# Two conditioned attention layers: batches pipelined over half-query sub-groups, scores from float32r pieces on row halves

## The chip, the cores and the metric

The kernel runs on one core of a Trainium2 chip. The metric is the device time of one execution in microseconds. The median of three runs of the kernel before is 675.55 us (675.35 to 675.59).

## The reference

Two layers run one after the other on x, of 2 batches x 1024 tokens x 256 channels in float32. The first is softmax attention with 16 heads of 16 channels, the second a linear attention with 8 heads of 32 channels.

```python
# layer 0, 16 heads of 16
xn = layer_norm(x, norm_w, norm_b)
q, k = heads(xn @ q_w + q_b), heads(xn @ k_w + k_b)
att = softmax(einsum('bnhl,bmhl->bnmh', q, k) + (1 - mask) * -1e6, axis=2)
v = heads((xn @ v_w + v_b) * mask)
y = einsum('bnmh,bmhl->bnhl', att, v)
scale, shift = split(silu(cond) @ emb_w + emb_b)
x = x + silu(layer_norm(y) * (1 + scale) + shift) @ out_w + out_b
# layer 1, 8 heads of 32
xn = layer_norm(x, ln_w, ln_b)
q = softmax(heads(xn @ Wq + bq), axis=-1)
k = softmax(heads(xn @ Wk + bk + (1 - mask) * -1e6), axis=tokens)
v = heads((xn @ Wv + bv) * mask)
y = q @ (k.T @ v)                       # per head
x = x + silu(layer_norm(y) * (1 + scale1) + shift1) @ W_out + b_out
```

## The kernel before

The program is written engine by engine; each engine runs its own list in the order in which it is written, and semaphores join the lists. All DMAs are issued by SyncE's queue (SPq).

**Preparation.** For both batches in turn: the input norm on VectorE (`layer_norm`, L708 statistics, L722 normalise), transposes on TensorE (L491), scale and bias on ScalarE (L391, into `hT`), then the q and k projections of 4 head groups (L500, 128x512 float32 matmuls; `product` is the helper with line 500 for all projections) and the values. Each q,k unit is split into three bfloat16 pieces: ScalarE L406, VectorE L788, ScalarE L408, GpSimd L356. SPq writes the pieces of a group to DRAM (L297, L304) and reads them back as `qs` and `ks` (L280 to L282, the function `stack`), so that six products of pieces, the mask rows and the row maxima stand under each other in one operand of 102 rows.

**Attention.** There are 8 groups (2 batches x 4 groups of 4 heads). For each group the maxima of the scores are found first: 64 matmuls of 99 rows x 512 columns (L519) into two PSUM banks `sN`, and 64 VectorE reductions of 128x512 out of PSUM (L749). The negated maxima are transposed (L528), split (L738 to L744) and brought by DMA into the last rows of `qs` (`load_max`, L288 and L290), so that the next matmul, L581, gives scores minus maximum. Its 128x1024 unit is turned by ScalarE into probabilities (L425, `prob`), and L539 multiplies these with the values, four 32-column tiles of the array at a time, in float32. While group g is attended, the maxima of group g+1 are found: `ring_plan` spreads them between the score matmuls. The maxima of group 0, and half of those of group 1, come before the first score (`prologue`). L433 copies the sums, L524 transposes them, L757 and L759 divide.

**After the attention.** Layer norm, the output projection and the whole of layer 1 run stage by stage, both batches in turn in each stage; L851 adds into `xs`, and SPq stores `xs` (L329). The projection of `cond` (L552) is made in the last group.

## Time and profile before

| | us |
|---|---|
| median of the runs | 675.55 |
| span of the profiled execution | 674.4 |
| start to the first score's exponential | 110 |
| attention, to the last values | 414 |
| the rest of layer 0 and layer 1, to the end | 151 |
| TensorE busy | 589.8 |
| VectorE busy | 470.1 |
| ScalarE busy | 347.5 |

Times of single instructions come from the one profiled execution. A matmul in the trace lasts from its start to the end of its way through the array, so in a stream neighbours overlap: what one costs there is the distance between starts. A float32 matmul appears as two instructions.

### The profile page before, as it was taken

What the parts mean: (1) busy time and instruction counts of PE and PEld (TensorE: products, weight loads), DVE (VectorE), ACT (ScalarE), POOL (GpSimd) and SP (SyncE); (2) the same over time, 40 slices, a digit from 0 to 9 for tenths busy, and PEclk for the clock granted to TensorE, in tenths of its full rate; (3) what the DMA queues carried; (4) which work ended last, traced back from release to release, by engine and by line L of the source; (5) the groups of instructions that cost most, each with busy time, mean ns of one, the idle gap of its engine ahead of it and who ended that gap; (6) DMA issues with size and microseconds to landing.
All of it is one profiled execution on the core that took longest, in us unless ns stands there. A gap on an engine that the chain in (4) does not pass through costs nothing.

```text
span 674.4 us, 9341 instructions
## 1 busy us (share of the span) xinstructions
PE 589.8 (87%) x2922; PEld 241.6 (36%) x2922; DVE 470.1 (70%) x905; ACT 347.5 (52%) x409; POOL 53.5 (8%) x42
## 2 busy tenths in 40 slices
PE   1989888999999999999999999999889666999666
PEld 1464412222222222222222222222234553588655
DVE  4639996888788788788888788888020547585652
ACT  1565304564655656656656655656976421538021
POOL 7224600000000000000000000000000005000000
PEclk9999955999999999999999999999989896999969
DMA  8188801500600600600410330100000000000003
GB/s 228 51 142 205 338 21 31 65 0 4 96 1 3 95 0 3 93 2 3 70 25 3 52 43 3 57 7 3 2 1 1 0 0 1 0 1 1 0 1 124
DMA packets 20021, 29.95 MB, mean 44 GB/s; under 512 B 5202, under 2 KB 11556, under 8 KB 19844
## 3 DMA queue, kind: packets, MB, share of 16 engines
q1 hardware_dynamic: 19996, 29.62, 20.8%
q8 instruction: 15, 0.25, 0.2%
q14 instruction: 10, 0.08, 0.0%
HBM read 21.02 MB, written 8.60 MB: 44 GB/s over the span
## 4 chain that ended last, share of the span: by engine, by line
PE 62%; DVE 23%; ACT 9%; issue 4%; DMA 1%; SPq 0%; DVEq 0%; ACTq 0%
PE bank L539 18%; PE bank L519 15%; DVE halfmax L749 15%; PE bank L500 14%; PE bank L581 11%; ACT work L391 3%; DVE stats L708 2%; ACT work L425 2%; DVE y_all L788 1%; PE bank L552 1%; DVE work L722 1%; DVE parts L722 1%; PE bank L524 1%; ACT parts L408 1%; DMA vecs<-in_mask_BxS_ff 1%
## 5 line engine op out<-in xcount | busy, mean ns | idle before, releaser
L749 DVE TENSOR_REDUCE halfmax<-bank 128x1 f32<-128x512 f32 x512 | 325.7, 688 | 63.7 <-PE bank L519 63.5
L425 ACT ACTIVATE work<-bank 128x1024 f32<-128x1024 f32 x256 | 250.0, 1023 | 152.6 <-PE bank L581 152.3
L519 PE MATMUL bank<-ks,qs 99*128 (+1 forms) x512 | 202.9, 404 | 17.1 <-DVE halfmax L749 11.0
L581 PE MATMUL bank<-qs,ks 102*128 (+1 forms) x512 | 167.6, 386 | 7.9 <-ACT work L425 5.4
L539 PE MATMUL bank<-work,vs 128*32 128x512 f32 x1024 | 137.0, 608 | 0.4 <-ACT yT L433 0.4
L519 PEld LDWEIGHTS bank<-ks,qs 99*128 (+1 forms) x512 | 49.7, 97 | 228.4 <-DVE halfmax L749 125.3
L581 PEld LDWEIGHTS bank<-qs,ks 102*128 (+1 forms) x512 | 47.5, 100 | 61.2 <-ACT work L425 18.5
L500 PE MATMUL bank<-parts,work 128*128 128x256 f32 x192 | 44.6, 393 | 7.1 <-ACT work L391 7.1
L500 PEld LDWEIGHTS bank<-parts,work 128*128 128x128 f32 x192 | 37.7, 198 | 13.4 <-ACT work L391 7.6
L367 POOL COPY vs<-v_all 128x512 f32 (+1 forms) x8 | 4.9, 612 | 396.8 <-PE bank L539 396.8
L500 PE MATMUL bank<-work,y_all 128*128 128x512 f32 x64 | 30.9, 624 | 2.4 <-ACT work L391 2.4
L539 PEld LDWEIGHTS bank<-work,vs 128*32 128x32 f32 x1024 | 20.4, 108 | 34.2 <-issue 30.8
L851 DVE TENSOR_TENSOR xs<-xs,bank 128x512 f32<-128x512 f32 x16 | 11.0, 687 | 26.5 <-PE bank L500 26.5
L788 DVE SCALAR_TENSOR_TENSOR y_all<-bank,cols,parts 128x512 f32<-128x512 f32 x16 | 12.0, 749 | 15.2 <-ACT parts L406 15.2
L384 ACT ACTIVATE std<-var 128x8 f32<-128x8 f32 x8 | 1.7, 209 | 39.9 <-DVE var L713 39.9
L500 PE MATMUL bank<-work,parts 128*128 128x512 f32 x32 | 15.9, 653 | 6.7 <-ACT work L391 6.7
L356 POOL TENSOR_TENSOR parts<-y_all,parts 128x512 f32 x16 | 18.5, 1155 | 37.7 <-ACT parts L408 37.7
L491 PE MATMUL bank<-ident,parts 128*128 128x128 f32 x48 | 9.1, 366 | 13.7 <-DVE parts L722 12.5
L500 PE MATMUL bank<-wo,work 128*128 128x256 f32 x64 | 16.0, 413 | 4.5 <-ACT work L391 4.5
L391 ACT ACTIVATE work<-bank,modB,modA 128x512 f32<-128x512 f32 x16 | 11.1, 777 | 16.4 <-PE bank L491 16.4
L826 DVE TENSOR_TENSOR emb<-bank,cols 128x8 f32<-128x8 f32 x2 | 0.2, 162 | 27.2 <-PE bank L552 27.2
L491 PE MATMUL bank<-ident,work 128*128 128x128 f32 x80 | 11.3, 303 | 8.1 <-DVE work L722 7.4
(119 smaller groups left out, 406.1 us busy)
## 6 DMA issues: line engine op xcount, KB each, us to landing
part_rows<-parts SPq DMA_DIRECT2D x8, 768.0 KB, 5.0
qs<-part_rows SPq DMA_DIRECT2D x48, 128.0 KB
ks<-part_rows SPq DMA_DIRECT2D x48, 128.0 KB
xs<-in_x SPq DMA_DIRECT2D x2, 1024.0 KB, 6.1
out_x<-xs SPq DMA_DIRECT2D x4, 512.0 KB, 2.9
parts<-in_L_cond_emb_w SPq DMA_DIRECT2D x1, 1024.0 KB, 5.6
parts<-in_L_cond_W_emb SPq DMA_DIRECT2D x1, 1024.0 KB, 7.9
ks<-in_mask_BxSx_fk SPq DMA_DIRECT2D x1, 1024.0 KB, 4.8
```

The source lines that it names most:

```text
L356: pool.tensor_tensor(parts[:, b * HG + hg, 2, n * HALF:(n + 1) * HALF], rest[:, u % 2, :], parts[:, b * HG + hg, 1, n * HALF:(n + 1) * HAL ...
L391: act.activation(hT[b][:, kc, q * HALF:(q + 1) * HALF], B8[i], func, scale=A(kc), bias=Bc(kc)).then_inc(turn_read, 1)
L425: act.activation(prob[:, c % 2, j, :], sT[u % 2][:, :], ACT.Exp).then_inc(exp_done, 1)
L491: last = pe.transpose(o[:, t * P:(t + 1) * P], z[:, 4 * q + t, kc * P:(kc + 1) * P], ident[:, :])
L500: last = pe.matmul(o, l, r, start=(i == 0), stop=(i == len(terms) - 1))
L519: pe.matmul(o, qs[0:ROW_MAX, slot, j, qt * P:(qt + 1) * P], ks[0:ROW_MAX, slot, j, n * HALF:(n + 1) * HALF], start=True, stop=True).then_i ...
L539: last = pe.matmul(acc[32 * j:32 * j + 32, n * HALF:(n + 1) * HALF], vs[:, c, j, :], prob[:, c % 2, j, n * HALF:(n + 1) * HALF], start=(c ...
L581: last = pe.matmul(sT[u % 2][:, n * HALF:(n + 1) * HALF], ks[0:ROWS, slots[0], j, c * P:(c + 1) * P], qs[0:ROWS, slots[0], j, n * HALF:(n ...
L708: dve.bn_stats(stats[:, b, t, :], src(t)).then_inc(ln_step, 1)
L722: dve.tensor_scalar(dst, s, mv[:, b, t, 0:1], rstd[:, b, t:t + 1], op0=ALU.subtract, op1=ALU.mult).then_inc(z_ready, 1)
L749: dve.tensor_reduce(halfmax[:, r, n:n + 1], src, axis=AX.X, op=ALU.max, negate=True).then_inc(sN_read, 1)
L788: dve.scalar_tensor_tensor(out=rest[:, u % 2, :], in0=B8[4 + u % 4], scalar=cols[:, c:c + 1], in1=parts[:, b * HG + hg, 0, n * HALF:(n + 1 ...
```

## The change

The program is rewritten around one loop of 128 steps.

- **Pieces.** q and k are split into two float32r pieces instead of three bfloat16 ones: ScalarE writes the first, VectorE the second, and GpSimd no longer takes part. Three products of pieces, two mask rows and two maximum rows make 52 rows (50 for the maxima), so a head fits into 64 partitions. Heads 0 and 2 of a group lie on partitions 0 to 63 of `qs` and `ks`, heads 1 and 3 on 64 to 127, and matmuls come in pairs, one on each half, into two banks. A piece is float32 in DRAM; a group is brought in by 20 DMAs instead of 13.
- **Sub-groups.** A group is cut into two halves of 512 queries. A sub-group has 8 steps, one for each 128 keys; a step holds two score pairs (L782), two 128x1024 exponentials, the values of the step before (L799) and four matmuls for the maxima (L682), which run 40 maxima ahead. The counts of all of these are those of the kernel before: 512 score matmuls, 512 maxima, 256 exponentials, 512 value matmuls. The ring of banks for maxima and all side work has three banks instead of two; the value sums have one.
- **Pipelining.** Only batch 0 is prepared before the loop. The preparation of batch 1, the projection of `cond`, and, once the groups of batch 0 are done, the rest of layer 0 and all of layer 1 for batch 0 are placed in single steps by the table `begins`; a projection is cut into two parts, one in each half of a step. Behind the loop stands batch 1's rest of layer 0 and layer 1.
- **Moved work.** The square root of the norms becomes a power on GpSimd, which also normalises four of the eight norms (L503). Biases of queries and values are added by a matmul with ones (L667) instead of VectorE. In the loop, SiLU is one 128x2048 instruction of its own (L564).
- The maxima go straight from SBUF to `qs` by two DMAs, without DRAM. SPq issues the first of these after the stacks of groups 1 and 2 and the weights of layer 1.

The core of the diff:

```diff
-    Q_PART = [0, 0, 0, 1, 1, 2]
-    K_PART = [0, 1, 2, 0, 1, 0]
-    PARTS = 3
+    Q_PART = [0, 0, 1]
+    K_PART = [0, 1, 0]
+    PARTS = 2
+    TILE = P // 2
+    SUBS = G * NH
+    STEPS = SUBS * NT
+    QT = HALF // P
+    MAXES = GH * QT * NH
+    AHEAD = MAXES + 8
...
+        stream = [("max", s, m) for s in range(SUBS) for m in range(MAXES)]
+        def maxima(k, p):
+            at = AHEAD + 4 * k + 2 * p
+            return stream[at:at + 2]
+        for (hg, n), k in zip([(hg, n) for hg in range(HG) for n in range(NH)], (4, 5, 7, 8, 19, 20, 21, 23)):
+            begins["qk", 1, hg, n] = (k, 0)
+        for s, k in enumerate((10, 11, 12, 13)):
+            begins["v", 1, s] = (k, 0)
+        for l in range(2):
+            begins["emb", l] = (15 + l, 0)
+            begins["embT", l] = (17 + l, 1)
+        for s in range(SUBS - 1):
+            begins["y", s] = (NT * (s + 1) + 1, 1)
+            begins["neg", s + 1] = (NT * (s + 1) - 2, 0)
...
+        for u, k in enumerate((88, 90, 91, 92)):
+            begins["keys", 0, u] = (k, 0)
+        for s, k in enumerate((93, 95, 96, 98)):
+            begins["queries", 0, s] = (k, 0)
+        for s, k in enumerate((99, 100, 101, 103)):
+            begins["values", 0, s] = (k, 0)
...
+        pe_first = [("T", "in0", 0, i) for i in range(4)] + [("qk", 0, hg, n) for hg in range(2) for n in range(NH)]
+        pro_rest = [("qk", 0, 2, 0), ("qk", 0, 2, 1), ("qk", 0, 3, 0), ("qk", 0, 3, 1)] + [("v", 0, s) for s in range(4)]
+        pe_beside, dve_beside = [], []
+        for i in range(AHEAD):
+            if i % 4 == 3 and i // 4 < len(pro_rest):
+                pe_beside.append(pro_rest[i // 4])
+            pe_beside.append(stream[i])
+            if i == MAXES + 1:
+                pe_beside.append(("neg", 0))
+            dve_beside.append(stream[i])
+            if i % 4 == 1 and 1 <= i // 4 and pro_rest[i // 4 - 1:] and pro_rest[i // 4 - 1][0] == "qk":
...
-            for g in range(HG):
-                sp.wait_ge(part3_ready, (g + 1) * NH)
-                sp.dma_start(part_rows[g], parts[:, g]).then_inc(parts_out, 16)
-                if g < 2:
-                    sp.wait_ge(parts_out, 16 * (g + 1))
-                    stack(g, g)
-                    sp.wait_ge(stack_in, (g + 1) * 16 * STACKS)
-            for g in range(HG, G):
-            load_max(0, 0)
...
+                    sp.wait_ge(rows_ready, 4 * (slot + 1))
+                else:
+                    sp.wait_ge(sT_ready, 2 * NT * NH * (g - SLOTS + 1))
+                sp.wait_ge(parts_out[g % 2], 16 * (g // 2 + 1))
+                for two in range(2):
+                    for r, part in enumerate(Q_PART):
+                        src = part_rows[g, 0:GC, part, :].rearrange("(c two p) n -> two p c n", two=2, p=DH0)[two]
+                        for n in range(NH):
+                            sp.dma_start(qs[two * TILE + r * DH0:two * TILE + (r + 1) * DH0, slot, n, :, :].bitcast(F32),
+                                         src[:, :, n * HALF:(n + 1) * HALF]).then_inc(stack_in[slot], 16)
+                    for r, part in enumerate(K_PART):
+                        src = part_rows[g, GC:2 * GC, part, :].rearrange("(c two p) n -> two p c n", two=2, p=DH0)[two]
+                        sp.dma_start(ks[two * TILE + r * DH0:two * TILE + (r + 1) * DH0, slot, :, :].bitcast(F32), src).then_inc(stack_in[slot], 16)
...
+            store_parts(0)
+            stack(0)
+            sp.dma_start(wo0[:, :, :], out_w.rearrange("(k p) c -> p k c", p=P)).then_inc(wo_in, 16)
             for i, src in enumerate((emb_w, W_emb)):
                 sp.dma_start(embw[:, i], src.rearrange("(e p) c -> p e c", p=P)).then_inc(embw_in, 16)
+            for g in range(1, HG):
+                store_parts(g)
+            stack(1)
+            stack(2)
             for i, src in enumerate((Wq, Wk, Wv, W_out)):
+                sp.dma_start(w1[:, i], src.rearrange("(k p) c -> p k c", p=P)).then_inc(w1_in, 16)
+            load_mrow(0)
+            load_max(0)
+            for k in range(STEPS):
+                for g in range(HG, G):
+                    if k == begins["qk", 1, g % HG, 1][0] + 2:
+                        store_parts(g)
+                if k % NT == NT - 2 and k // NT + 1 < SUBS:
+                    load_max(k // NT + 1)
+                if k % (NT * NH) == 0 and SLOTS <= k // (NT * NH) + 2 < G:
+                    stack(k // (NT * NH) + 2)
...
-                            last = pe.matmul(sT[u % 2][:, n * HALF:(n + 1) * HALF], ks[0:ROWS, slots[0], j, c * P:(c + 1) * P],
-                                             qs[0:ROWS, slots[0], j, n * HALF:(n + 1) * HALF], start=True, stop=True)
-                            if n == NH - 1:
-                                last.then_inc(sT_ready, 1)
...
+            def scores(k, u):
+                s, g, n, c = where(k)
+                if u == 0 and c == 0:
+                    pe.wait_ge(cmax_in, 32 * (s + 1))
+                if k > 0:
+                    pe.wait_ge(exp_done, 2 * (k - 1) + u + 1)
+                for two in range(2):
+                    rows = slice(two * TILE, two * TILE + ROWS)
+                    last = pe.matmul(sT[u][:, two * HALF:(two + 1) * HALF], ks[rows, g % SLOTS, u, c * P:(c + 1) * P],
+                                     qs[rows, g % SLOTS, n, u, :], start=True, stop=True)
+                last.then_inc(sT_ready, 1)
...
+                for j in range(GH):
+                    last = pe.matmul(acc[32 * j:32 * j + VW, :], vp[:, b, c, hg * GH + j, :], prob[:, c % 2, j, :],
+                                     start=(c == 0), stop=(c == NT - 1), skip_group_check=True)
...
+            for k in range(STEPS):
+                scores(k, 0)
+                for key in maxima(k, 0):
+                    fill(key, 0)
+                for key, part in pe_at[k, 0]:
+                    fill(key, part)
+                scores(k, 1)
+                if k > 0:
+                    values(k - 1)
+                for key in maxima(k, 1):
+                    fill(key, 0)
+                for key, part in pe_at[k, 1]:
+                    fill(key, part)
...
-                    pe.matmul(o, qs[0:ROW_MAX, slot, j, qt * P:(qt + 1) * P], ks[0:ROW_MAX, slot, j, n * HALF:(n + 1) * HALF],
-                              start=True, stop=True).then_inc(sN_ready, 1)
...
+                    rows = slice(two * TILE, two * TILE + ROW_MAX)
+                    last = pe.matmul(o, qs[rows, g % SLOTS, n, c, t * P:(t + 1) * P], ks[rows, g % SLOTS, c, half * HALF:(half + 1) * HALF], start=True, stop=True)
...
+                for kc in range(KC):
+                    last = pe.matmul(o[:, part * D:(part + 1) * D], hT[:, kc, at], w[:, kc, :], start=(kc == 0), stop=(kc == KC - 1 and row is None))
+                if row is not None:
+                    last = pe.matmul(o[:, part * D:(part + 1) * D], ones[:, :], brow[:, row, :], start=False, stop=True)
...
-                    dve.scalar_tensor_tensor(out=rest[:, u % 2, :], in0=B8[4 + u % 4], scalar=cols[:, c:c + 1],
-                                             in1=parts[:, b * HG + hg, 0, n * HALF:(n + 1) * HALF],
-                                             op0=ALU.add, op1=ALU.subtract).then_inc(pj_read, 1)
...
+                    dve.scalar_tensor_tensor(out=staged[:, 1, :].bitcast(F32R), in0=o, scalar=cols[:, COL["qk_b"] + hg:COL["qk_b"] + hg + 1], in1=staged[:, 0, :],
+                                             op0=ALU.add, op1=ALU.subtract).then_inc(u.done, 1)
...
-                    pool.tensor_tensor(parts[:, b * HG + hg, 2, n * HALF:(n + 1) * HALF], rest[:, u % 2, :],
-                                       parts[:, b * HG + hg, 1, n * HALF:(n + 1) * HALF], op=ALU.subtract).then_inc(part3_ready, 1)
...
+                for t in range(NT):
+                    pool.tensor_scalar(z[:, t, :], source(kind, b, t), rstd[:, L, t:t + 1], shift[:, L, t:t + 1], op0=ALU.mult, op1=ALU.add).then_inc(z_ready[kind, b], 1)
...
+                    act.activation(hT[:, :, :], hT[:, :, :], ACT.Silu).then_inc(silu_ready[key[1:]], 1)
```

TensorE inside the attention of the kernel before (L519 maxima, L581 scores, L539 values):

```order
L519 MATMUL bank<-ks,qs 128x512
L581 MATMUL bank<-qs,ks 128x512 x2
L519 MATMUL bank<-ks,qs 128x512
L581 MATMUL bank<-qs,ks 128x512
L519 MATMUL bank<-ks,qs 128x512
L539 MATMUL bank<-work,vs 32x512 x4
```

TensorE in a step of the changed kernel with no side work but the transposes of finished values (L682 maxima, L782 scores, L799 values, L691 transposes):

```order
L782 MATMUL sT<-qs,ks 128x512 x2
L682 MATMUL bank<-ks,qs 128x512 x2
L782 MATMUL sT<-qs,ks 128x512 x2
L799 MATMUL bank<-prob,vp 17x512 x4
L682 MATMUL bank<-ks,qs 128x512 x2
L691 MATMUL bank<-ident,yT 128x128 x4
```

The single maxima between scores have become pairs, and four matmuls of the maxima, four of the scores and one block of values still make a step.

TensorE in step 10 of the changed kernel, where values of batch 1 are projected (L665 with `wv`, L667 the bias):

```order
L782 MATMUL sT<-qs,ks 128x512 x2
L682 MATMUL bank<-ks,qs 128x512 x2
L665 MATMUL bank<-wv,hT 128x256 x2
L667 MATMUL bank<-brow,ones 128x256
L782 MATMUL sT<-qs,ks 128x512 x2
L799 MATMUL bank<-prob,vp 17x512 x4
L682 MATMUL bank<-ks,qs 128x512 x2
L665 MATMUL bank<-wv,hT 128x256 x2
L667 MATMUL bank<-brow,ones 128x256
```

In the kernel before, projections stood ahead of the attention; six float32 matmuls of 256 columns now stand among the scores of one step.

SPq before the first maxima DMA, in the kernel before (from the stack of group 1 on):

```order
L280 DMA qs<-part_rows 16x4x1024 x6
L280 DMA ks<-part_rows 16x4x1024 x6
L282 DMA ks<-mask_rows 3x4x1024
L297 DMA part_rows<-parts 128x3072 x2
L304 DMA part_rows<-parts 128x3072 x4
L308 DMA parts<-in_L_cond_emb_w 128x4x512
L308 DMA parts<-in_L_cond_W_emb 128x4x512
L310 DMA parts<-in_L_cond_Wq 128x2x256
L310 DMA parts<-in_L_cond_Wk 128x2x256
L310 DMA parts<-in_L_cond_Wv 128x2x256
L310 DMA parts<-in_L_cond_W_out 128x2x256
L288 DMA max_rows<-cparts 32x3x128
```

SPq in the changed kernel, from behind the stack of group 0 to the first maxima DMA (L420); the second of the two stacks, with the same rows as the first, and the last three weights are not shown:

```order
L442 DMA late<-in_L_cond_W_emb 128x4x512
L394 DMA part_rows<-late 128x2048 x3
L407 DMA qs<-part_rows 16x2x512 x6
L411 DMA ks<-part_rows 16x2x1024 x3
L412 DMA ks<-mask_rows 2x2x1024
...
L448 DMA w<-in_L_cond_Wq 128x2x256
...
L427 DMA late<-in_mask_BxSx_fk 128x1024
L420 DMA qs<-crows 2x8x128 x4
```

Two whole stacks, 40 DMAs, and five large loads now stand ahead of the first maxima.

## Rows read from the trace of the kernel before

**Rows 1.** The page: busy time, share of the span and instructions of each engine.

```profile
PE 589.8 (87%) x2922; PEld 241.6 (36%) x2922; DVE 470.1 (70%) x905; ACT 347.5 (52%) x409; POOL 53.5 (8%) x42
```

**Rows 2.** Busy time by stretch; columns as the first line says.

```profile
core 0: us, PE busy (x) PEld busy (x) DVE busy (x) ACT busy (x) POOL busy (x), PEclk, DMA share, GB/s
97.00:109.00 12.00, 10.04 (x19) 1.96 (x19) 10.78 (x20) 0.03 (x1) 0.00 (x0) 0.50 0.02 5
109.00:523.00 414.00, 391.70 (x2092) 110.28 (x2090) 301.76 (x530) 259.68 (x267) 4.29 (x7) 0.99 0.18 27
...
221.51:274.82 53.31, 50.56 (x266) 13.83 (x265) 43.62 (x74) 32.13 (x33) 0.62 (x2) 1.00 0.22 31
```

**Rows 3.** Timeline of two score units, mid attention: start, duration, engine, line, idle before.

```profile
250.20 0.39 PE L519 MATMUL bank<-ks,qs 99*128 x1
...
250.52 1.06 PE L539 MATMUL bank<-work,vs 128*32 128x512 f32 x8
...
251.51 0.39 PE L519 MATMUL bank<-ks,qs 99*128 x1
...
251.74 0.38 PE L581 MATMUL bank<-qs,ks 102*128 x1
...
251.94 2.54 DVE L749 TENSOR_REDUCE halfmax<-bank 128x1 f32<-128x512 f32 x4 [0.54 <-PE bank L519]
251.96 0.38 PE L519 MATMUL bank<-ks,qs 99*128 x1
251.96 0.32 PEld L581 LDWEIGHTS bank<-qs,ks 102*128 x2
252.18 0.60 PE L581 MATMUL bank<-qs,ks 102*128 x2
252.59 1.94 ACT L425 ACTIVATE work<-bank 128x1024 f32<-128x1024 f32 x2 [1.07 <-PE bank L581]
...
253.61 1.06 PE L539 MATMUL bank<-work,vs 128*32 128x512 f32 x8
```

**Rows 4.** Groups by form: count, busy us, mean ns of one, idle before.

```profile
L749 DVE TENSOR_REDUCE halfmax<-bank 128x1 f32<-128x512 f32 x512 | 325.7, 688 | 63.7 <-PE bank L519 63.5
...
L500 PE MATMUL bank<-parts,work 128*128 128x256 f32 x192 | 44.6, 393 | 7.1 <-ACT work L391 7.1
...
L500 PE MATMUL bank<-work,y_all 128*128 128x512 f32 x64 | 30.9, 624 | 2.4 <-ACT work L391 2.4
...
L356 POOL TENSOR_TENSOR parts<-y_all,parts 128x512 f32 x16 | 18.5, 1155 | 37.7 <-ACT parts L408 37.7
...
L788 DVE SCALAR_TENSOR_TENSOR y_all<-bank,cols,parts 128x512 f32<-128x512 f32 x16 | 12.0, 749 | 15.2 <-ACT parts L406 15.2
...
L500 PE MATMUL bank<-att,qs 128*128 128x128 f32 x32 | 3.7, 275 | 0.0
...
L673 PE MATMUL bank<-ident,parts 128*128 128x128 f32 x16 | 1.9, 272 | 0.0
```

**Rows 5.** Waits of SPq from 26 to 47 us: total, times, longest.

```profile
SPq L297 <- DMA ks<-mask_rows: 7.6, 1, 7.6
...
SPq L280 <- DMA part_rows<-parts: 2.9, 1, 2.9
```

**Rows 6.** Timeline of the start, SPq: start, duration of the issues.

```profile
29.23 0.36 SPq L297 DMA_DIRECT2D part_rows<-parts  x1
32.51 2.69 SPq L280 DMA_DIRECT2D qs<-part_rows  x6
35.24 2.77 SPq L280 DMA_DIRECT2D ks<-part_rows  x6
```

**Rows 7.** The chain that ended last, behind the attention: start, duration, what.

```profile
527.73 1.28 ACT L391
529.03 2.80 ACT work L391 x4
531.87 8.86 PE bank L500 x32
...
544.04 7.19 PE bank L500 x32
551.94 2.63 DVE stats L708 x8
555.96 2.67 DVE parts L722 x8
```

1344 lines of the change are left out of this document (699 added, 645 removed).

## The prediction

> **What bounds the kernel now.** I read the shares of the engines first: TensorE is busy for 87% of the span, VectorE for 70% [rows 1]. The stretches then say where: the attention takes 414 us of the 674.4 [rows 2], and a steady group in it 53.3 us, of which TensorE is busy 50.6, VectorE 43.6 and ScalarE 32.1. The timeline of two score units [rows 3] says what one round costs. From one values block to the next are 3.09 us. The block takes 0.99 to the start of the next matmul, and its start comes 0.32 after the maximum before it, 0.10 more than the 0.22 between neighbours: 1.09 with the change of tile shape. Eight bfloat16 matmuls at 0.22 make 1.76. So TensorE has 2.85 of work, and the missing 0.24 is time in which VectorE had not yet freed one of two banks. VectorE needs 2.51 for its four reductions (four take 2.54, the last 0.03 of it is latency; 0.627 each), ScalarE 1.94 for two exponentials. TensorE is the bound, VectorE stands 0.34 behind it.
>
> **The attention step.** Counts stay: per step four maxima, four score matmuls, one values block, two exponentials. What changes on TensorE is that the eight matmuls become four pairs on row halves. No row shows float32r, nor a matmul on half the rows. Bounds for a pair: 0.22, if a float32r piece streams like bfloat16 and the halves run together, as the four column tiles of a values block do (eight instructions of 512 columns in 0.99); 0.44, if one half follows the other; and 0.95, if they follow each other at the rate of a float32 transpose, one pass of 128 columns in 0.119 [rows 4] or 0.475 for 512. I take 0.25, near the lower end, because the tiles of the values block are the nearest rows for two tiles at a time, and because the trace's plain float32 matmul shows two instructions where float32r has one. TensorE then has 4 x 0.25 + 1.09 = 2.09 in a step, and VectorE with 2.51 becomes the bound. Two engines then stand close, so a wait remains; with three banks I take half of the 0.24 of [rows 3], 0.12, with 0 and 0.24 as its ends.
>
> A page speaks against the pairs: the Trainium skill, "TensorE: Matmul & The Clock Gate", Part 3, says that a weight load overlaps a matmul in flight only when their row groups differ. The trace disagrees for whole rows: a load of 102 rows begins at 251.96 together with a matmul of 99 rows [rows 3], and two loads take 0.32, the second starting 0.22 after the first, so 0.10 each. By the rule a pair would take 0.22 + 0.10 = 0.32, a quiet step 2.37 on TensorE, still below 2.51, and the steps bound by TensorE together some 11 us more.
>
> **Side work in the loop.** Prices: a float32 matmul of 256 columns is two instructions of 0.225 (32 in 7.19 us, [rows 7]; 0.232 in [rows 4]), so 0.45, one of 512 columns 0.9, one of 128 columns 0.23 (3.7/32 twice), a transpose 0.12 [rows 4]. For each of the 128 steps I add what the table puts there on TensorE, VectorE and ScalarE, and take the largest:
> - 84 steps without projections: VectorE, 84 x 2.51 = 211, and 46 us of its small work in them (finishing the maxima, dividing y, statistics, splits at 0.75 [rows 4]): 257.
> - 20 steps with a projection of two 512-column matmuls, or four of 256: TensorE 2.09 + 1.8 = 3.9 (less in the last four, which have no maxima): 77.
> - 12 steps with layer 0 or layer 1 values, or queries: six matmuls of 256, because of the bias matmul, 2.09 + 2.7 = 4.8: 57.
> - 5 steps with the projection of `cond`, the k.T v product or y: 26.
> - 2 steps with the SiLU: 128x2048 on ScalarE, 1.9 by the exponential's rate, and two table loads of 1.28 [rows 7], beside 1.9 of exponentials, 6.3 each: 13.
> - 5 steps without maxima or projections: ScalarE, 13.
> Sum 443. To it: 128 x 0.12 = 15 of waits. Batch 1's first norm: statistics, then GpSimd's power and its eight normalising instructions (half of the 1.155 of a 512-column one each, [rows 4]), stand in steps 1 to 3, while TensorE's transposes in steps 2 and 3 already wait for them, with all later scores queued behind: about 5. Every float32 projection between pairs adds two changes of tile shape; about 110 fall into steps that TensorE bounds. Between 0 and 0.10 each, I take 0.04: 5. The loop is 443 + 15 + 5 + 5 = 468.
>
> The Trainium skill, "TensorEngine Tiling (Array Packing)", Key Properties, says that each change of the tiling mode drains the engine. At the 0.10 of [rows 3] the 110 changes would cost 11 instead of 5, which would make the loop 474.
>
> **Ahead of the loop.** Until the first q,k unit little changes. The third piece is gone, two stages of a unit less, so the store of group 0 goes out at about 26 instead of 29.2 [rows 6] and lands 3 to 4 later (2.9 of waiting behind a 0.36 issue, [rows 5], for 768 KB; now 1 MB). The stack of group 0 took 13.6 us before, from 32.5 to 46.1 (issues to 38.4, 7.6 of waiting, [rows 5, 6]). Its bytes are the same, 1.5 MB, its issues are 20 at 0.45 = 9. I take 12 to 13: the first maximum runs at about 43. Then 40 maxima with 8 projections: four rounds of 0.75 + 2.51 on VectorE (13) and four on TensorE of 2.7 + 1.1 (15), then 5 for the rest: 78, the maxima of the first sub-group being ready at 76. But SPq stores group 3 only after its last q,k unit, at 57, then issues two stacks (40 x 0.45 = 18) and the five loads (3): the first maxima DMA is issued at 78. In front of it in the same queue lie 3.2 MB of stacks at 12 to 13 per stack, hence until 57 + 25 = 82, and 1.5 MB of loads, 4 to 6. First score at 88, between 80 and 94, against 110 before. All engines idle for that wait; it is new.
>
> **Behind the loop.** One batch instead of two, so its latencies are bare:
> - last values, copy 1.0, transposes, division: 3; statistics 2.6 [rows 7], aggregation 1.1, power 0.7, half a normalisation 1.3, transposes, table load 1.3, two ScalarE units 1.4: 9.
> - output projection 8.9, the cold one of [rows 7] (the second, 7.2).
> - add, statistics, norm, ScalarE: 7. Keys 8.6.
> - Queries and values 2 x 24 matmuls x 0.45 = 21.6, transposes 3.9, k.T v 32 x 0.23 / 2 = 3.7, waits 1, y 3.7: 34.
> - norm 8, projection 8.9, add and the store 4.5.
> Sum 92, of which some 3 overlap: 89, between 82 and 97.
>
> The span is 88 + 468 + 89 = 645, and with the 1.15 by which the median stands above the span of the profile, 646: 0.956 of before.
>
> **The rivals.**
> - The halves don't run together, or stream at half the rate together: a pair costs 0.44. For it: no row shows two row groups at work. Then TensorE stays the bound with 4 x 0.44 + 1.09 = 2.85 in a step, exactly as before, and the projections come on top of it. The largest of each step sum to 486; with waits of 0.12 to 0.24 and the 10 above, 511 to 527, total 689 to 705. Slower by 2 to 4%. It decides from a pair of about 0.37 up: each 0.01 of a pair above 0.35 costs 3 to 5 us.
> - float32r streams at the transpose's rate, one half after the other, 0.95 a pair: TensorE's sum is 492 pairs x 0.95 + 128 x 1.09 + 99 of side work = 706, total near 890.
> - The waits are as large as now, and the first score is at 94: 646 + 15 + 6 = 667. Same direction, half the gain.
> - Everything tight: pairs at 0.22, no waits, no drains, the start at 82 and the end at 84: 441 + 5 + 166 + 1 = 613.
> - The clock. The granted clock fell to 0.50 where TensorE only waited between single maxima from 97 to 109 us [rows 2]; it stayed at 0.99 in the attention. A step with 2.09 of work in 2.63 lies between the two. At half clock a quiet step costs 4.2 on TensorE and the loop over 680, but TensorE would then be busy throughout, so I give it little.
>
> **How the numbers follow.** The forecast, 630 to 660, has 0.50; everything tight 0.08; the larger waits, 660 to 674, 0.13; halves in turn 0.20, of which 0.03 lands within 0.2% of before; float32r slow 0.06; the clock 0.03. Faster 0.70, same 0.05, slower 0.25; 0.2% is about what three runs can tell from no change. The range reaches from 616 to 705 and leaves out the slow float32r, the clock and half of the tight case.
>
> **What would show it.** Two matmuls of a pair starting within 0.05 us of each other, and the next pair 0.25 later; VectorE at 2.5 of 2.65 in a quiet step, waiting for TensorE in steps 10 to 13 and 93 to 103; the first exponential at 88 with an idle VectorE for some 10 us before it, released by a DMA; a hole of about 5 us in step 2; 89 us behind the last exponential. If TensorE is busy above 95% in quiet steps, the pairs are what failed.

## The result, and the profile after

The changed kernel takes 746.3 us (median of four runs, 742.45 to 757.94), 1.1025 times the kernel before (95% interval 1.0986 to 1.1064). The longest of the four, which had the lowest mean clock, is left out of the ratio. 646 was predicted, inside 616 to 705: the direction is wrong, the forecast is missed by 100 us and the range by 41. The profiled execution has a span of 746.4 us, so its sums can be set against the forecast's directly.

The page's busy times, in the columns of [rows 1]:

```profile
PE 605.8 (81%) x2986; PEld 277.8 (37%) x2986; DVE 448.5 (60%) x878; ACT 350.2 (47%) x399; POOL 81.6 (11%) x77
...
PEclk9959955999999898997986999899999999978997
```

None of the three busy engines is nearer to its limit than before: TensorE falls from 87 to 81%, VectorE from 70 to 60%. The row of the granted clock has new dents in the middle. By stretch (first exponential at 107.5 us, last one done at 653), in the columns of [rows 2]:

```profile
0.00:107.50 107.50, 46.87 (x143) 25.19 (x145) 48.55 (x84) 15.93 (x24) 31.05 (x29) 0.84 0.66 151
107.50:653.30 545.80, 492.16 (x2513) 196.58 (x2511) 357.50 (x682) 307.97 (x335) 41.09 (x44) 0.92 0.13 27
653.30:746.40 93.10, 66.79 (x332) 55.99 (x332) 42.45 (x112) 26.27 (x41) 9.46 (x4) 0.85 0.04 12
```

| stretch | predicted | measured | difference |
|---|---|---|---|
| to the first score's exponential | 88 | 107.5 | +19.5 |
| the loop | 468 | 545.8 | +78 |
| behind the loop | 89 | 93.1 | +4 |

**A quiet step.** The timeline of one step of the loop without side work (start, duration, engine, line, idle before; L682 maxima, L782 scores, L799 values, L922 VectorE's maximum out of a bank, L625 the exponential):

```profile
269.87 0.50 PE L682 MATMUL bank<-ks,qs 50*128 50x512 f32 x2
270.20 0.39 PE L782 MATMUL sT<-qs,ks 52*128 52x512 f32 x2
270.40 2.48 DVE L922 TENSOR_REDUCE halfmax<-bank 128x1 f32<-128x512 f32 x4 [0.42 <-PE bank L682]
270.44 0.39 PE L682 MATMUL bank<-ks,qs 50*128 50x512 f32 x1
271.15 0.50 PE L682 MATMUL bank<-ks,qs 50*128 50x512 f32 x1 [0.32 <-DVE halfmax L922]
271.15 0.72 PE L782 MATMUL sT<-qs,ks 52*128 52x512 f32 x2
271.80 1.05 PE L799 MATMUL bank<-prob,vp 128*17 128x512 f32 x8
271.91 1.02 ACT L625 ACTIVATE prob<-sT 128x1024 f32<-128x1024 f32 x1 [0.24 <-PE sT L782]
272.78 0.50 PE L682 MATMUL bank<-ks,qs 50*128 50x512 f32 x2
```

From maxima to maxima are 2.91 us, in most steps 2.92 to 2.94, where 2.63 was forecast; VectorE works 2.48 of them and then waits 0.42 for TensorE. The rows name a ring of waits. The fourth maximum cannot start before 271.15, when VectorE frees the first bank; behind it in TensorE's list stand the second score pair and the values, until 272.78; only then come the two maxima that VectorE needs next. VectorE ran out of banks meanwhile, because three banks cannot cover 0.65 us of scores and 0.98 of values.

The same rows show what a pair costs. The first pair behind the values is followed by the next start after 0.33 (269.87 to 270.20), and so is the first behind a wait (271.15 to 271.48, inside the second row of scores); the pair behind another pair is followed after 0.23 (270.20 to 270.44). Of the 0.71 from 270.44 to 271.15, 0.23 are one matmul and about 0.47 the wait. Without it TensorE's list of a quiet step therefore takes some 2.44 us, an estimate from these starts, where 2.09 was forecast: still under VectorE's 2.51, but close to it.

**The clock.** At the seventh step of each sub-group the negated maxima are transposed (L686). Timeline of one such step and of the matmuls after it:

```profile
253.50 1.28 DVE L922 TENSOR_REDUCE halfmax<-bank 128x1 f32<-128x512 f32 x2
253.69 0.09 PEld L686 LDWEIGHTS bank<-ident,cpieces 128*32 128x32 f32 x1 [1.11 <-DVE halfmax L922]
253.72 0.27 PE L686 MATMUL bank<-ident,cpieces 128*32 128x128 f32 x1 [0.83 <-DVE cpieces L930]
...
254.35 1.36 PE L799 MATMUL bank<-prob,vp 128*17 128x512 f32 x8
...
256.47 2.48 DVE L922 TENSOR_REDUCE halfmax<-bank 128x1 f32<-128x512 f32 x4 [1.51 <-PE bank L682]
...
258.36 1.91 PE L799 MATMUL bank<-prob,vp 128*17 128x512 f32 x8
```

TensorE stands still for 0.83 us until VectorE has finished and split the maxima, in front of scores and values that need nothing from it. The values block then takes 1.36 and in the next step 1.91 instead of 1.05: the clock has fallen. The windows around two of these steps say so:

```profile
235.00:254.90 19.90, 17.63 (x109) 6.21 (x101) 17.59 (x33) 13.53 (x15) 0.00 (x0) 1.00 0.13 54
255.10:261.70 6.60, 6.60 (x25) 2.31 (x21) 3.15 (x6) 2.67 (x4) 0.00 (x0) 0.50 0.16 51
261.90:282.20 20.30, 17.78 (x108) 6.43 (x112) 17.54 (x32) 13.69 (x15) 0.00 (x0) 1.00 0.49 63
282.40:289.00 6.60, 6.60 (x29) 2.31 (x21) 2.80 (x6) 2.66 (x3) 0.00 (x0) 0.50 0.01 2
```

0.50 is the lower of TensorE's two levels, 1.2 instead of 2.4 GHz, and a quiet step takes 4.56 there. In all 82.6 us of the loop ran at it; by the quiet step, 2.93 against 4.56, that is about 82.6 x 0.36 = 30 us lost, an estimate, since other steps slow by another share. The longest of these stretches, 25 us, is the start of the loop, behind the 14 us in which TensorE waited for the DMA of the first maxima. The clock also spreads the executions: one at a mean clock of 0.917 took 742.5 us, one at 0.887 took 757.9.

### The profile page after: what moved, and what is told of

The parts are those of the page before. It is cut to its first block, busy times and chain, and to the rows that moved or that the text cites. A ratio compares the mean times of both kernels' runs of the same rounds, so it can differ in the third digit from the quotient of the medians.

```text
span 746.4 us, 7987 instructions
## 1 busy us (share of the span) xinstructions
PE 605.8 (81%) x2986; PEld 277.8 (37%) x2986; DVE 448.5 (60%) x878; ACT 350.2 (47%) x399; POOL 81.6 (11%) x77
## 4 chain that ended last, share of the span: by engine, by line
PE 55%; DVE 23%; issue 8%; SPq 4%; DMA 4%; ACT 3%; POOL 2%; POOLq 0%; DVEq 0%; ACTq 0%
PE bank L799 16%; DVE halfmax L922 14%; PE bank L682 13%; PE sT L782 7%; PE bank L665 7%; DVE z L877 2%; SPq L407 2%; PE bank L704 2%; DVE stats L855 2%; PE sT L704 2%; DMA qs<-crows 2%; PE bank L697 1%; PE bank L667 1%; ACT prob L625 1%; SPq L411 1%
## 5 line engine op out<-in xcount | busy, mean ns | idle before, releaser
L922 DVE TENSOR_REDUCE halfmax<-bank 128x1 f32<-128x512 f32 x512 | 323.9, 683 | 192.8 <-PE bank L682 192.6
L625 ACT ACTIVATE prob<-sT 128x1024 f32<-128x1024 f32 x256 | 260.5, 1024 | 198.1 <-PE sT L782 197.0
L682 PE MATMUL bank<-ks,qs 50*128 50x512 f32 x512 | 176.0, 504 | 39.8 <-DVE halfmax L922 19.5
L782 PE MATMUL sT<-qs,ks 52*128 52x512 f32 x512 | 143.9, 488 | 16.4 <-DMA qs<-crows 14.2
L682 PEld LDWEIGHTS bank<-ks,qs 50*128 50x128 f32 x512 | 74.2, 198 | 205.6 <-DVE halfmax L922 109.1
L799 PE MATMUL bank<-prob,vp 128*17 128x512 f32 x1024 | 147.5, 650 | 0.4 <-ACT prob L625 0.3
L782 PEld LDWEIGHTS sT<-qs,ks 52*128 52x128 f32 x512 | 58.8, 199 | 64.9 <-issue 53.1
L665 PE MATMUL bank<-w,hT 128*128 128x256 f32 x144 | 39.9, 404 | 4.6 <-issue 2.1
L799 PEld LDWEIGHTS bank<-prob,vp 128*17 128x17 f32 x1024 | 17.2, 96 | 42.6 <-issue 25.1
L665 PEld LDWEIGHTS bank<-w,hT 128*128 128x128 f32 x144 | 25.9, 193 | 17.3 <-issue 9.4
L667 PE MATMUL bank<-brow,ones 128*128 128x256 f32 x64 | 19.0, 379 | 0.0
L507 POOL TENSOR_TENSOR xs<-xs,bias_rows 128x2048 f32<-128x2048 f32 x4 | 18.1, 4528 | 3.0 <-DVE z L877 2.8
L665 PE MATMUL bank<-wo,hT 128*128 128x256 f32 x64 | 16.5, 399 | 2.0 <-ACT hT L564 1.7
```

The costliest lines, as they stand in the source:

```text
L507: pool.tensor_tensor(xs[:, b * NT:(b + 1) * NT, :], xs[:, b * NT:(b + 1) * NT, :], bias_rows[:, row:row + 1, :].to_broadcast([P, NT, D]), ...
L625: act.activation(prob[:, c % 2, 2 * u:2 * u + 2, :].rearrange("p j n -> p (j n)"), sT[u][:, :], ACT.Exp).then_inc(exp_done, 1)
L665: last = pe.matmul(o[:, part * D:(part + 1) * D], hT[:, kc, at], w[:, kc, :], start=(kc == 0), stop=(kc == KC - 1 and row is None))
L667: last = pe.matmul(o[:, part * D:(part + 1) * D], ones[:, :], brow[:, row, :], start=False, stop=True)
L682: last = pe.matmul(o, qs[rows, g % SLOTS, n, c, t * P:(t + 1) * P], ks[rows, g % SLOTS, c, half * HALF:(half + 1) * HALF], start=True, sto ...
L782: last = pe.matmul(sT[u][:, two * HALF:(two + 1) * HALF], ks[rows, g % SLOTS, u, c * P:(c + 1) * P], qs[rows, g % SLOTS, n, u, :], start=T ...
```

## The experiments

The ratios are to the kernel before on the same chip. "The five sub-groups" are the 40 steps 24 to 63, without projections.

### What the wait for the first score is made of

`z` of batch 0 (L877 on VectorE) took 12.39 us while GpSimd cleared `qs` and `ks`; timeline of the kernel after:

```profile
12.80 12.39 DVE L877 TENSOR_SCALAR z<-xs,mv,rstd 128x256 f32<-128x256 f32 x8 [1.24 <-POOL rstd L487]
...
12.98 1.97 POOL L480 MEMSET qs<- 32x2048 f32 x1
```

**e1_memsets_later**

```diff
             pool.wait_ge(ones_ready, 1)
+            pool.wait_ge(z_ready["in0", 0], NT)
             unit_rows(1)
```

> GpSimd fills the constant rows of the second and third slot only after the first norm is written, instead of beside it. Theory A (GpSimd's memsets slow VectorE's normalisation, 12.4 us for eight instructions against 2.7 before): they take 2.7 again, everything after them up to the first score comes 9 to 10 us earlier, and the total falls by about 10 us, to 736. Theory B (the eight are slow for another reason, such as late data): they still take over 10 us and the total stays at 746.

Measured: 737.3 us, 1.0924 (1.0901 to 1.0946), first exponential at 99.9, 7.6 earlier. The same instructions of e1_memsets_later:

```profile
12.88 2.67 DVE L878 TENSOR_SCALAR z<-xs,mv,rstd 128x256 f32<-128x256 f32 x8 [1.24 <-POOL rstd L487]
```

The eight instructions fall from 12.39 to 2.67 although the memsets are only moved: the two engines hindered each other, VectorE by a factor of 4.6, GpSimd by little (its memsets of `qs` took 1.97 and 1.84 beside VectorE, and 1.80 without it). The Trainium skill, "GPSIMD Engine Reference", Key points, says that GpSimd shares its SBUF interfaces with VectorE and contends with some of its instructions; the trace agrees, and gives the price. Of the 9.7 us saved, 7.6 reach the first score, and the total falls by 9.0, as theory A said.

**e2_maxima_dma_first**

```diff
             stack(1)
+            load_max(0)
             stack(2)
...
-            load_max(0)
```

> The DMA of the first maxima is issued between the stacks of group 1 and group 2 instead of behind both and behind five loads. Theory A (the first score at 106.7 waits for this DMA, which waits for what stands before it in the queue, while the maxima were ready at 90.9): the first score runs at about 94 and the total falls by 12 us, to 734. Theory B (the later start of the stack of group 2 and the weights is paid back in the loop): the first score is earlier, but the total falls by less than 4.

Measured: first exponential at 96.5, 11 us earlier. The total, 738.05 (722.24 to 747.22 in four runs), does not settle how much of that remains: the mean clock was 0.895 in the profiled execution and 0.941 in the shortest. The start is confirmed, the total left to the combination below.

### What holds the quiet step

**e3_one_and_three**: one maximum in the first half of a step, three in the second.

```diff
-            at = AHEAD + 4 * k + 2 * p
-            return stream[at:at + 2]
+            at = AHEAD + 4 * k
+            return stream[at + 1:at + 4] if p else stream[at:at + 1]
```

> Of the four maxima of a step one stands in the first half and three in the second, so no maximum that has to wait for a bank stands directly ahead of the values block. Theory A (a quiet step takes 2.92 us because the second maximum waits for the reduction of the third of the step before, and the scores and the 1 us values block queue behind it): the quiet step falls to 2.6 to 2.7, near VectorE's 2.5, and the total by 15 to 22 us, to about 727. Theory B (the step is bound by TensorE's own work or by its hand-over with ScalarE): the quiet step stays at 2.9 and the total within 5 us of 746.

Measured: 789.4 us, 1.1618 (1.1522 to 1.1714). The quiet step stayed at 2.93, so theory A's cure fails; the median step with a q,k unit rose from 5.47 to 5.89, one with six matmuls of 256 columns from 6.1 to 6.8. The trace tells why. TensorE of e3_one_and_three:

```profile
269.52 0.73 PE L682 MATMUL bank<-ks,qs 50*128 50x512 f32 x3
269.86 0.62 PE L782 MATMUL sT<-qs,ks 52*128 52x512 f32 x2
270.80 0.50 PE L682 MATMUL bank<-ks,qs 50*128 50x512 f32 x1 [0.32 <-DVE halfmax L922]
270.80 0.73 PE L782 MATMUL sT<-qs,ks 52*128 52x512 f32 x2
```

One maximum still waits 0.32 for a bank with a score pair and the values behind it. For the quiet step it does not matter how the four are dealt out; that a waiting one stands in front of work that is ready does, as the next run shows.

**e8_scores_first**: both score pairs at the head of a step.

```diff
                 scores(k, 0)
+                scores(k, 1)
                 for key in maxima(k, 0):
...
-                scores(k, 1)
```

> Both score pairs of a step stand ahead of the first two maxima; the second maximum, which waits for a bank, is then followed by the values block alone. The theory after the run with one and three maxima, whose quiet step stayed at 2.93 because a waiting maximum still stood ahead of scores and values: the quiet step is a loop of the next maximum's way to VectorE (0.54), its reduction (0.63), the release (0.12), the second score pair (0.65) and the values block (0.99), together 2.93. Without the score pair the loop is 2.3 to 2.4, so VectorE's 2.5 binds: the quiet step falls to 2.6, the total by 15 to 25 us at equal clock. Rival (TensorE's own streams bind, or the scores then wait for ScalarE): the quiet step stays within 0.1 of 2.9.

Measured: 701.8 us, 1.0379 (1.0347 to 1.0410), 44.5 less than after. TensorE and VectorE of e8_scores_first in one step:

```profile
302.62 0.49 PE L682 MATMUL bank<-ks,qs 50*128 50x512 f32 x2
...
302.95 0.64 PE L782 MATMUL sT<-qs,ks 52*128 52x512 f32 x4
303.14 2.48 DVE L922 TENSOR_REDUCE halfmax<-bank 128x1 f32<-128x512 f32 x4 [0.18 <-PE bank L682]
...
303.42 0.97 PE L682 MATMUL bank<-ks,qs 50*128 50x512 f32 x2
...
304.32 1.05 PE L799 MATMUL bank<-prob,vp 128*17 128x512 f32 x8
...
305.31 0.50 PE L682 MATMUL bank<-ks,qs 50*128 50x512 f32 x2
```

The step is 2.69 and VectorE waits 0.18 in it. So VectorE is the bound with two moved matmuls, as the forecast had it, and the order within a step was what kept it from being so. The clock gained too: 39.4 us of the loop at the lower level instead of 82.6, at 0.36 some 16 of the 46 us by which the loop shortened. The other 30 are waits by this estimate, 20 of them the 0.24 of each of the 84 quiet steps. That is more than the 15 to 25 expected at equal clock.

**e5_scores_twice**: each score pair is computed twice, the second time over the first.

```diff
-                for two in range(2):
+                for two in (0, 1, 0, 1):
```

> Every score pair is computed twice in a row with the same result, so TensorE has about 0.25 more work in each half step and nothing else changes. Theory A (the half clock comes from how little of a quiet step TensorE works): the stretches at 0.5 between 240 and 400 us vanish, the mean clock rises from 0.90 to 0.94 or more, and the total is within 15 us of 746 although 512 matmuls are added. Theory B (it comes from single waits, or the halves don't overlap): the clock stays near 0.90 and the total rises by 45 to 70 us.

Measured: 763.1 us, 1.1281. The quiet step becomes 3.17, 0.24 more for two more pairs. Only the pair in front of the values lies on the ring. TensorE of e5_scores_twice there:

```profile
303.89 0.96 PE L782 MATMUL sT<-qs,ks 52*128 52x512 f32 x4
304.79 1.05 PE L799 MATMUL bank<-prob,vp 128*17 128x512 f32 x8
```

From the waiting maximum's start to the values are 0.90 us instead of 0.65, so a pair behind another costs 0.24, near the 0.25 of the forecast. The loop's time at the lower clock fell to 31 us, though, by 51; at 0.36 this gives back some 18 of what the added work cost. Theory A comes close: the mean clock is its 0.94 and one stretch of 4 us at 0.5 is left between 240 and 400 us, but the total is 17 us above 746 and not within 15.

**e7_same_half**: the order of the pieces is altered so that the two maxima of a pair lie on the same row half.

```diff
-            return m // 4 % 2, m % 2, m // 8, m // 2 % 2
+            return m // 4 % 2, m // 2 % 2, m // 8, m % 2
```

> The changed kernel with the order of the maxima's pieces altered, so that the two score pieces of a pair lie on the same row half instead of on the two. Theory A (the halves run at the same time, as the equal starts in the trace of after say): such a pair then takes about 0.43 us instead of 0.22 to 0.33, TensorE's work in a quiet step grows by 2 x 0.2, and the quiet step from 2.93 to 3.05 to 3.3, the total from 746 to 765 to 790. Theory B (the equal starts are a matter of how the records are written, and the halves gain nothing): step and total stay within 0.05 and 10 us.

Measured: 760.3 and 783.8 us, too far apart for a total (the mean clock is 0.901 in the first and 0.867 in the second, the profiled one). Steps with a projection of two 512-column matmuls rose from 5.47 to 5.70, quiet ones stayed at 2.93. Neither theory gets its number. TensorE of e7_same_half shows why:

```profile
346.08 0.50 PE L782 MATMUL sT<-qs,ks 52*128 52x512 f32 x2
346.41 0.80 PE L682 MATMUL bank<-ks,qs 50*128 50x512 f32 x2
346.71 0.73 PE L782 MATMUL sT<-qs,ks 52*128 52x512 f32 x2
...
348.36 0.49 PE L682 MATMUL bank<-ks,qs 50*128 50x512 f32 x1
348.37 0.50 PE L782 MATMUL sT<-qs,ks 52*128 52x512 f32 x1
```

A maximum no longer starts with its partner but with the score matmul behind it, which lies on the other half (348.36 and 348.37). Any neighbours on different halves pair up; only where a projection cuts the row is the partner missing, and there a lone maximum costs about 0.23. That the halves run together holds; in the kernel after the two matmuls of a pair start 0 to 5 ns apart.

### What the clock costs

**e9_transpose_later**: the transpose of the maxima one half-step later.

```diff
-            begins["neg", s + 1] = (NT * (s + 1) - 2, 0)
+            begins["neg", s + 1] = (NT * (s + 1) - 2, 1)
```

> The transpose of the finished maxima stands half a step later, so TensorE no longer waits about 0.8 us for VectorE's three small instructions ahead of scores and values in the seventh step of each sub-group (5.0 us now at full clock). Theory A (this wait, and the wait for the copy behind it, are what the granted clock falls on in the middle of the loop): the seventh step falls to 3 to 4 us, fewer stretches at 0.5 between 240 and 400 us, the total 10 to 25 us less. Theory B (the clock falls for the low density of a quiet step as a whole): the seventh step gets shorter by 1, but the stretches at 0.5 stay; total less by 10 or under.

Measured: 726.6 us, 1.0735 (1.0702 to 1.0768), 20 less than after. Theory A holds: the seventh step takes 3.70, no stretch at 0.5 is left between 133 and 403 us, and the total fell by its 10 to 25. The quiet step is unchanged, 2.93. One window row each for the five sub-groups, in the order after, e9_transpose_later, e8_scores_first, e5_scores_twice:

```profile
234.50:369.70 135.20, 122.32 (x666) 43.22 (x663) 105.53 (x190) 84.65 (x87) 0.00 (x0) 0.90 0.19 34
```

```profile
233.60:357.80 124.20, 111.59 (x667) 40.25 (x665) 106.85 (x191) 83.32 (x86) 0.00 (x0) 1.00 0.21 37
```

```profile
225.40:341.20 115.80, 109.06 (x667) 42.07 (x664) 105.61 (x190) 80.38 (x87) 0.00 (x0) 1.00 0.22 40
```

```profile
241.40:378.20 136.80, 130.06 (x826) 54.19 (x822) 105.79 (x190) 84.69 (x86) 0.00 (x0) 0.99 0.19 34
```

TensorE's busy share is 0.90 in both of the first two (122.3 of 135.2, 111.6 of 124.2), yet the clock fell in one and held in the other. What differs is where the wait for VectorE's splits stands. That wait alone does not bring the clock down either: in these five sub-groups e8_scores_first and e5_scores_twice keep it in full, 4.2 us over five times as in the kernel after, and the clock held at 1.00 and 0.99, with TensorE busy for 0.94 and 0.95. The falls came where the wait met the lower busy share.

The kernel before needs 53.31 for two such sub-groups [rows 2], 26.7 each; the kernel after 27.0, e9_transpose_later 24.8, e8_scores_first 23.2. So the changed kernel gains nothing even where no projection is in the way; with the transpose later it gains 7%, and with the scores first 13%. Of the 11.0 us between the first two rows most is the clock: the seventh step took 4.22 where the clock held (step 62) and takes 3.70 now, so the wait itself is some 2.6 of the five sub-groups.

### What the moved preparation costs

**e4_parts_together**: both parts of a projection in the same half-step.

```diff
             if key[0] in TWO_PARTS:
-                at = later(at)
                 pe_at[at].append((key, 1))
+                at = later(at)
```

> Both parts of a projection stand behind each other in one half of a step instead of one in each half. Theory A (a float32 projection between pairs costs a change of tile shape in and out, and holds one of three banks between its parts, so the maxima in between wait): the steps with projections, 5.5 and 5.8 us now, get 0.4 to 0.9 shorter, 37 of them, and the total falls by 15 to 30 us. Theory B (what counts is how long VectorE is left without a maximum): a block of 1.9 to 2.8 us starves it longer, and the total rises by 5 to 20 us.

Measured: 768.2 us in the one run at a mean clock of 0.915, and 787.5 to 794.2 in three at 0.873 to 0.885, so no ratio is given; the total rose by 22 or more, a little above theory B's 5 to 20. A step with a q,k unit rose from 5.47 to 5.89, one with values from 5.83 to 6.5: VectorE starves behind two parts in a row (for 3.59 us before 171.91), and the price depends on the place, not only on the sum.

**e6_prep_later**: the preparation of batch 1 four steps later.

```diff
-        for i, at in enumerate([(2, 0), (2, 1), (3, 0), (3, 1)]):
+        for i, at in enumerate([(6, 0), (6, 1), (7, 0), (7, 1)]):
...
-        for s, k in enumerate((10, 11, 12, 13)):
+        for s, k in enumerate((13, 15, 16, 18)):
```

(and the q,k units and the projection of `cond` likewise)

> The transposes of batch 1's first norm stand in steps 6 and 7 instead of 2 and 3, and the projections behind them some four steps later. Theory (GpSimd's power of 1.7 us and its normalisation stand between VectorE's statistics in steps 1 and 2 and transposes in steps 2 and 3, and all scores queue behind them): step 2, 14.8 us now, falls to 5 or less, the rest pays at most 3 back, the total falls by 8 to 12 us at equal clock. Rival: the wait only moves to step 6.

Measured: 746.7 us, 1.1038, no gain. The hole in front of batch 1's transposes does close: step 2 falls from 14.8 to 4.6 us. In the kernel after TensorE stands there for GpSimd, 7.52 us:

```profile
118.35 1.66 POOL L487 TENSOR_TENSOR rstd<-var,neghalf 128x8 f32<-128x8 f32 x1 [84.00 <-DVE var L868]
...
120.40 4.32 POOL L503 TENSOR_SCALAR z<-xs,rstd,shift 128x256 f32<-128x256 f32 x8
...
122.71 1.09 PE L697 MATMUL bank<-ident,z 128*128 128x128 f32 x4 [7.52 <-POOL z L503]
```

But part of it comes back at the new place (steps 6 and 7 take 10.2 instead of 9.1), the projections meet other small work, and the time at the lower clock stays, 83.6 us against 82.6. Which of these takes how much was not separated.

**e10_values_before_parts**: e8_scores_first, and the values go ahead of the first part. In e8_scores_first TensorE stood 0.78 us in front of a first part for a bank, with the values behind it:

```profile
212.80 1.12 PE L704 MATMUL bank<-hT,wqk 128*128 128x512 f32 x2 [0.78 <-DVE halfmax L922]
...
213.85 1.05 PE L799 MATMUL bank<-prob,vp 128*17 128x512 f32 x8
```

```diff
                 for key in maxima(k, 0):
                     fill(key, 0)
-                for key, part in pe_at[k, 0]:
-                    fill(key, part)
                 if k > 0:
                     values(k - 1)
+                for key, part in pe_at[k, 0]:
+                    fill(key, part)
```

> Both scores first, as in e8_scores_first, and besides the step's eight value matmuls are issued ahead of its first projection part instead of behind it. Theory A (three banks): in e8_scores_first TensorE stood 0.78 us in front of the first part of each step with two 512-column parts, for a bank that VectorE had not yet reduced, and the 1.05 us of values waited behind it although their exponentials were long done; with the values in that gap a step with two 512-column parts falls from 5.28 to about 4.5, one with two 256-column parts from about 4.5 to 4.0, quiet steps stay at 2.69, and some 40 steps give 20 to 28 us: 675 to 682. Theory B (the gap is a debt of VectorE, not of the order): the part waits as long behind the values, or the next maxima do, the step stays within 0.2 of 5.28 and the total within 6 us of e8_scores_first (701.8).

Measured: 689.2 us, 1.0189 (1.0158 to 1.0220), 12.6 less than e8_scores_first. TensorE of e10_values_before_parts in such a step:

```profile
205.93 1.05 PE L799 MATMUL bank<-prob,vp 128*17 128x512 f32 x8
206.91 1.13 PE L704 MATMUL bank<-hT,wqk 128*128 128x512 f32 x2
```

The wait is gone: those steps fall from 5.28 to 4.48, as theory A said. The median step with six 256-column matmuls gained only 0.4 (5.7 to 5.3), so the sum of 20 to 28 was too high by half.

### Together

**e11_all_but_prep** is e10_values_before_parts with the edits of e1_memsets_later and e2_maxima_dma_first; **e12_all** adds that of e6_prep_later.

> e10_values_before_parts with the two changes ahead of the loop (GpSimd's memsets behind the normalised rows; the maxima's transfer between the second and third stack). If the parts of the loss add up: the first exponential comes at about 89 to 90 instead of 107 (7.6 and 11 us, each as measured alone), and the total is 17 to 19 us under e10_values_before_parts: 657 to 665 if theory A of that run holds, 680 to 685 if its theory B does. Rival: the stacks and the first loop steps take it back (GpSimd's batch-1 work then binds in step 2), and only 8 to 12 us remain.

Measured: 667.2 us, 0.9869 (0.9843 to 0.9895), 22.0 less than e10_values_before_parts; first exponential at 88.5, 20.5 earlier than in e10_values_before_parts. The two gains ahead of the loop add up.

> e11_all_but_prep with the preparation of batch 1 begun four steps later. With the clock settled by the fuller loop, theory A: step 2 (14 us in e8_scores_first, waiting for GpSimd's z) falls to about 5 and the total gains 8 to 11 us over e11_all_but_prep. Theory B: as in e6_prep_later, where step 2 fell from 14.8 to 4.6 but the total stayed at 746.7, the later parts meet steps that were quiet, the clock is at its lower level more often, and nothing is gained (within 4 us).

Measured: 662.2 us, 0.9801 (0.9769 to 0.9832): 84 us under the changed kernel and 2.0% faster than the kernel before. The gain on e11_all_but_prep is 5.0 us, between the two theories: step 2 falls from 12.5 to 4.1, and some of it returns in steps 6 and 7, which take 11.9 instead of 7.9. The windows of e12_all, in the columns of [rows 2]:

```profile
0.00:85.90 85.90, 45.88 (x143) 24.85 (x145) 38.85 (x84) 15.71 (x24) 30.61 (x29) 0.87 0.60 154
85.90:566.50 480.60, 455.42 (x2513) 191.88 (x2511) 360.93 (x682) 295.55 (x335) 41.15 (x44) 0.96 0.18 36
566.50:660.00 93.50, 67.22 (x332) 56.16 (x332) 42.45 (x112) 26.23 (x41) 9.46 (x4) 0.85 0.04 12
```

## Why the prediction was wrong

The same work, in another order within a step and at the start, takes 85.9 + 480.6 + 93.5 = 660 us, where 88 + 468 + 89 = 645 was forecast. The counts held, and so did most rates of single instructions; what failed was that each step was costed as the largest of three sums.

- **The pair, 0.25: right in kind, a little low in sum.** A pair behind another costs 0.24 (e5_scores_twice), but one behind the values or a wait 0.33, so TensorE's list of a quiet step takes 2.44 instead of 2.09. That left VectorE the bound, but with 0.07 to spare instead of 0.42. Of the expected signs, the two matmuls starting together came, and VectorE waits, though longer than foreseen. The rivals with slow pairs, which carried the slower cases, are refuted: the kernel is slower for another reason than the one named. The rival of the larger waits was of the right kind, but ended at 0.24 a step and 667 us.
- **"With three banks I take half of the 0.24": the step that failed first.** Measured 0.42 of waiting instead of 0.12, in the 84 quiet steps 35 us instead of 10. The wait was taken as a leftover of two engines standing close. It is a property of TensorE's order: a maximum that waits for a bank holds a score pair and the values. It should have been read from the order of the list, by following which release each instruction waits for. e8_scores_first brings the step to 2.69, 0.06 from the forecast.
- **The 84 quiet steps, 257 forecast, 313.5 measured (+56), in part the clock.** The rival was named and given 0.03, at the argument that TensorE at half clock would be busy throughout. That argument says that the clock comes back, not that it doesn't fall: it fell again and again, for 3 to 25 us of the loop at a time, and cost some 30 us in all by the estimate above. At 2.6 to 2.9 a step TensorE waits in every step, and the added wait of the seventh step came on top. Step 2, below, lies in this class too.
- **The side work, 0.9 for 512 columns: too low.** The 20 steps with two such matmuls took 99.9 instead of 77, the 12 with six of 256 columns 73.8 instead of 57, the other 12 took 58.6 instead of 52. One part costs 1.06 from start to start (212.80 to 213.85 above is 1.05), and the pairs cost the 0.35 of the first point: 3.9 becomes about 4.6 with both. The rest, up to 5.47 in a q,k step, is waiting for banks, and e10_values_before_parts, at 4.48, is rid of it by order alone. To assume the maximum of the engines' sums left that out.
- **GpSimd's norm in steps 1 to 3, 5 forecast: too low.** Step 2 took 14.8, and TensorE stood 7.5 of it waiting for GpSimd. The power of 128x8 elements takes 1.66 to 1.74 us and the eight instructions 4.32, and the clock was at its lower level all the while.
- These differences are 56.5 + 22.9 + 16.8 + 6.6 = 102.8; the 15, 5 and 5 of waits, norm and tile changes that the forecast added apart have to be taken off, and 78 remain.
- **First score, 88 forecast, 107.5 measured.** The store of group 0 was issued at 33.6 instead of 26, because of the 9.7 us that the memsets cost `z`, which the forecast did not price at all; without them it goes out at 24.5. That is 7.6 of the 19.5. The rest came after it: the first maximum ran at 53.2 instead of 43, and the store of group 3 was issued 18.3 behind it instead of 14, so the DMA of the maxima was issued at 94.2 instead of 78 and released the scores 12.5 later instead of 10. That it is queued behind two stacks was right in kind: e2_maxima_dma_first moves it and gains 11 us. Both edits together bring 88.5, but this is not the 88 of the forecast, which was for the order as it stood; there e1_memsets_later reaches 99.9.
- **Behind the loop, 89 forecast, 93.1 measured**: right within its bounds.

Open is how the 44.5 us of e8_scores_first divide between waits and clock better than by the 0.36 of a step at half clock, since neither can be held fixed while the other changes; and why e6_prep_later gives nothing alone but e12_all 5 us. Why a pair behind the values or a wait costs 0.33 was not tested, and neither was a fourth bank in the ring, for which this kernel has none left: four hold scores, one the value sums, three the ring.

## What to carry to other kernels

Before costing a loop as its busiest engine, write down the in-order list of the engine that feeds it and mark each instruction that waits for a release: whatever stands behind a waiting instruction and could run is paid as a gap on the next engine. Work that is ready (scores, values) goes ahead of work that waits for a buffer; here moving it gave 44.5 and 12.6 us without changing an instruction. When preparation moves under a loop, ask of each moved instruction what now runs at the same time on the shared memory and which waits of the loop it lengthens; and a change that turns TensorE from the bound into an engine that waits may cost clock as well.

## What the runs showed of the hardware

- Eight VectorE instructions of 128x256 float32 out of SBUF took 12.39 us beside GpSimd's memsets and 2.67 without them; the memsets of 32x2048 changed by little (1.83 to 1.97, and 1.80).
- Float32r matmuls of 50 to 52 rows on the two row halves mostly start within 0 to 5 ns of each other, from whichever neighbouring instructions they come. The next pair starts 0.33 later when the first follows the values block or a wait, and 0.23 to 0.24 later when it follows another pair; there its weight load (0.19, at 270.21) starts together with the matmuls before it.
- TensorE's granted clock fell to the lower level in a loop in which it was busy for 0.90 of the time, and held at the same share when one wait of 0.83 us, five times in 135 us, stood half a step later. It also held with the wait in place where TensorE was busy for 0.94 and 0.95. More work on the engine raised the clock: with every score pair computed twice, 31 us of the loop were at the lower level instead of 82.6.
- GpSimd's power of 128x8 elements took 1.66 to 1.74 us.
